# A Gram matrix of split halves from one doubled cross product in place of two

## What is computed

```python
h = relu(einsum('btd,edh->ebth', x, Wd1) + bd1[:, None, None, :])
recon = einsum('ebth,ehd->ebtd', h, Wd2) + bd2[:, None, None, :]
losses = mean((recon - x[None]) ** 2, axis=(2, 3))
idx = argmin(losses, axis=0)       # one expert of 8 for each batch
```

## Time and profile before

| | before |
| --- | --- |
| median of 3 runs | 2398.17 us (2398.06 to 2401.6) |
| the profiled execution's own time | 2398.65 us |
| its span, first to last instruction | 2396.9 us |
| mean granted TensorE clock | 0.972 |
| PE busy | 2142.2 us, 89% |
| DVE busy | 1480.8 us, 62% |
| ACT busy | 995.4 us, 42% |
| POOL busy | 661.0 us, 28% |

### The profile page before, as it was taken

One profiled execution on the slowest core, in us unless ns is written; L12 is line 12 of the kernel. 1 busy time (PEld: TensorE's weight loads), 2 busy tenths in 40 slices (PEclk: granted clock), 3 DMA queues, 4 the chain that ended last, 5 costly groups with the idle time before them and its releaser, 6 DMA issues.

```text
span 2396.9 us, 62050 instructions
## 1 busy us (share of the span) xinstructions
PE 2142.2 (89%) x26607; PEld 1403.2 (59%) x26607; DVE 1480.8 (62%) x3341; ACT 995.4 (42%) x1746; POOL 661.0 (28%) x902
## 2 busy tenths in 40 slices
PE   1589999999999999999999999999999999999955
PEld 1354756657475665747566574756657475565724
DVE  4466666575666667566666756666675666666531
ACT  1335344453534445354444535444453544445220
POOL 2112142231414223141322314132231413222041
PEclk9889999999999999999999999999999999999978
DMA  3312021120302103030210303021030302102010
GB/s 75 77 29 72 11 80 37 33 76 11 107 11 79 38 29 80 11 107 11 79 39 26 83 11 107 11 78 40 27 82 11 107 11 77 41 24 68 11 36 18
DMA packets 99866, 117.35 MB, mean 49 GB/s; under 512 B 19916, under 2 KB 70613, under 8 KB 99575
## 3 DMA queue, kind: packets, MB, share of 16 engines
q1 hardware_dynamic: 99592, 113.39, 17.8%
HBM read 36.99 MB, written 16.78 MB: 22 GB/s over the span
## 4 chain that ended last, share of the span: by engine, by line
PE 67%; DVE 13%; SPq 6%; ACT 6%; issue 3%; POOL 2%; DMA 1%; DVEq 1%; POOLq 0%; ACTq 0%
PE NS L865 10%; PE ringF L1081 10%; PE ringA L763 8%; PE ringF L1066 7%; SPq L373 6%; PE KV L946 5%; PE ringA L1032 5%; PE ringF L1114 3%; PE ringA L908 2%; DVE stage L1505 2%; PE ringA L932 2%; PE ringF L763 2%; PE ringF L1116 2%; ACT E L620 2%; PE ringF L1062 2%
## 5 line engine op out<-in xcount | busy, mean ns | idle before, releaser
L1081 PE MATMUL ringF<-x,H 128*128 128x257 f16 x1536 | 261.0, 273 | 0.0
L1429 DVE TENSOR_REDUCE mx<-ringA 128x8 f32<-128x512 f32 x256 | 175.6, 686 | 114.4 <-PE ringA L908 114.1
L1081 PE MATMUL ringF<-H 128*128 128x128 f16 x1536 | 233.7, 220 | 1.4 <-DVE H L1516 1.4
L612 ACT ACTIVATE E<-ringA,score_scale 128x512 f32<-128x512 f32 x256 | 175.3, 685 | 117.9 <-PE ringA L932 117.9
L763 PE MATMUL ringA<-xT,wqkv 128*128 128x512 f16 x768 | 177.9, 382 | 18.2 <-DMA KS<-KS 11.8
L620 ACT ACTIVATE E<-ringA,score_scale 128x512 f32<-128x512 f32 x256 | 158.6, 684 | 76.0 <-PE ringA L963 76.0
L1066 PE MATMUL ringF<-wd,x2T 128*128 128x512 f16 x768 | 190.0, 384 | 0.0
L1482 DVE SCALAR_TENSOR_TENSOR X<-X,NS 128x320 f32<-128x320 f32 x160 | 78.1, 488 | 180.7 <-PE NS L865 175.5
L1415 DVE TENSOR_REDUCE mx<-ringA 128x1 f32<-128x512 f32 x256 | 162.7, 684 | 31.3 <-PE ringA L899 31.0
L427 POOL TENSOR_SCALAR vtmp<-mv,eps_ffn 128x8 f32<-128x8 f32 x16 | 5.1, 316 | 628.1 <-DVE mv L1261 628.1
L427 POOL TENSOR_SCALAR vtmp<-mv,eps_ln 128x8 f32<-128x8 f32 x32 | 9.9, 310 | 608.6 <-DVE mv L1261 594.6
(11 more groups left out here) (251 smaller groups left out, 4634.2 us busy)
## 6 DMA issues: line engine op xcount, KB each, us to landing
KS<-stage SPq DMA_DIRECT2D x384, 64.0 KB, 2.0
QS<-stage SPq DMA_DIRECT2D x384, 64.0 KB, 2.0
xin<-in_L_attn_x_dram SPq DMA_DIRECT2D x16, 1024.0 KB, 6.8
xres<-in_L_attn_x_dram SPq DMA_DIRECT2D x16, 1024.0 KB, 7.9
out_dram<-yout SPq DMA_DIRECT2D x16, 1024.0 KB, 5.4
QS<-LB SPq DMA_DIRECT2D x16, 512.0 KB, 4.4
E<-in_L_attn_w_qkv_dram SPq DMA_DIRECT2D x1, 768.0 KB
E<-in_L_ffn_Wd_dram SPq DMA_DIRECT2D x2, 256.0 KB
```

Source lines behind the costliest of these rows:

```text
L612: A(E[:, k % ESLOTS, :], ps[:, :], ACT.Exp, scale=score_scale[:, 0:1]).then_inc(freed["s3"].sem, 1)
L1081: ins = MM(dst, H[:, a, t, own], src, start=first and i == 0, stop=last and i >= 4, skip_group_check=True)
L1429: V_.reduce_max(mx1[:, t, 8 * h:8 * h + 8], take(b, "m1", k)[:, :].rearrange("p (a m) -> p a m", a=8), AX.X)\
```

## The change

`H` gets a third plane. DVE's `hidden` gets a second instruction, which writes twice the high half there, and signals a new semaphore. PE's `gram` drops the matmul high by low, and in the matmul low by high the right operand is the doubled plane. PE waits once for the new semaphore, at the first tile of q = 0. As the sum against a symmetric matrix is the same for a matrix and its transpose, twice one cross product gives what the two gave.

```diff
-        H = sb("H", [P, 2, T, EH], F16)
+        H = sb("H", [P, 3, T, EH], F16)
...
+        h2 = sig("h2", T)
...
             def gram(b, q, tiles):
                 if q == 0 and 0 in tiles:
                     pe.wait_ge(freed["h"].sem, freed["h"].at(b, T))
+                    pe.wait_ge(h2.sem, h2.at(b, T))
...
-                            (0, ps[:, 0:P], H[:, 0, t, own]), (0, ps[:, 0:P], H[:, 1, t, own]),
+                            (0, ps[:, 0:P], H[:, 0, t, own]),
                             (0, ps[:, P:GR], x16[:, 0, t, 0:C + 1]), (0, ps[:, P:GR], x16[:, 1, t, 0:C + 1]),
-                            (1, ps[:, 0:P], H[:, 0, t, own]), (1, ps[:, P:GR], x16[:, 0, t, 0:C + 1]))):
-                        ins = MM(dst, H[:, a, t, own], src, start=first and i == 0, stop=last and i >= 4, skip_group_check=True)
+                            (1, ps[:, 0:P], H[:, 2, t, own]), (1, ps[:, P:GR], x16[:, 0, t, 0:C + 1]))):
+                        ins = MM(dst, H[:, a, t, own], src, start=first and i == 0, stop=last and i >= 3, skip_group_check=True)
...
                 V_.scalar_tensor_tensor(out=H[:, 1, t, :], in0=bank("h", t)[:, :], scalar=0.0, in1=H[:, 0, t, :],
                                         op0=ALU.max, op1=ALU.subtract).then_inc(freed["h"].sem, 1)
+                V_.tensor_scalar(H[:, 2, t, :], H[:, 0, t, :], 2.0, None, ALU.mult).then_inc(h2.sem, 1)
```

## The result

The changed kernel takes 2374.92 us (median of 4 runs, 2372.74 to 2376.48) against 2398.11 us before: a ratio of 0.9904, 95% interval 0.9891 to 0.9916, that is 20 to 26 us less. The forecast was 2378.4 us, 19.7 us less.

What follows compares the result with a forecast made beforehand. PE, busy 89%, was taken as the likely limit, but not in every stage. A gain of 25.1 us less a cost of 5.3 us gave 19.8 us, so 2378.4 us against the runs' median; range 2369 to 2386 us.

Steps and rivals of the forecast that it cites:

- Price of the removed matmul: PE's gram: each removed short matmul saves 0.0555 us by the spacing of starts, a half of four tiles 0.222 us.
- 81 ns for each removed pair: Rival in PE's gram: weight loads set the pace, so 36.6 us gained and 2366.9 us in all; chance 0.03.
- Seven halves of eight: Gram halves in 15 batches: all but the first half of gram(0) shorten the path, 23.3 us.
- covered half: First half of gram(0), ahead of the values' transposes: PE only waits longer for DVE, 0.46 not 0.24 us; no gain.
- Slack under the other halves: Iteration stage: the chains over DVE and ACT have 1.09 and 1.49 us spare against 0.22 us removed.
- Price of the added instruction: DVE's doubling of 128x512 f16: 285 ns long, by the slope of the f16 copy.
- step d: Time one doubling adds to DVE's stream: 0.20 us, with bounds 0.09 and 0.40.
- f32 rate: Rival on DVE's doubling: d is 0.40 us, cost 11.5 us, 2384.6 us in all; chance 0.09.
- Where it meets the path: Maxima stage: only hidden(4) with 0.14 us and hidden(7) with 0.20 us delay PE, 0.34 us a batch, 5.1 us.
- small waits at k = 4 and 5: Sign in the maxima stage: new small PE waits for DVE's reduction (L1429) appear there.
- The tail: After the last batch: 32 removed matmuls save 1.8 us, the last doubling ahead of the gram costs 0.2 us.
- The clock: Drops between 2.4 and 1.2 GHz in 13 of 15 batches may shift: -8.5 to +1.3 us, in the range only.

Runs made afterwards that it cites:

- doubled variant: The changed kernel with a second doubling of tiles 4 and 7 alone, into spare memory; 2382.8 us, ratio 0.9934 to the kernel before.
- kernel before with 5 and 3 tiles: The kernel before with the first pair's gram cut 5 and 3 tiles around the values' transposes, not 4 and 4; 2391.6 us, ratio 0.9971.
- DVE part alone: The kernel before with the doubled plane written and waited for, but all six matmuls a tile kept; 2401.3 us, ratio 1.001.
- two doublings moved: The changed kernel with the doublings of tiles 4 and 7 moved to places where DVE waits for PE; 2371.7 us, ratio 0.9886.
- the one with POOL: The changed kernel with all eight doublings given to POOL behind norm2, none on DVE; 2375.2 us, ratio 0.9906.

## Why the prediction was right

- **Price of the removed matmul.** 0.0555 us each and 0.222 us a half were predicted, so 1.55 us for seven halves; the iteration is 1.56 us shorter. After the change a tile's five matmuls start within 0.445 us. The order of time on PE shows one tile, from 1104.04 to the start of the next at 1104.49:

```profile
1104.04 0.23 PE L1083 MATMUL ringF<-H 128*128 128x128 f16 x1
1104.11 0.38 PE L1083 MATMUL ringF<-x,H 128*128 128x257 f16 x2
1104.33 0.22 PE L1083 MATMUL ringF<-H 128*128 128x128 f16 x1
1104.38 0.27 PE L1083 MATMUL ringF<-x,H 128*128 128x257 f16 x1
1104.49 0.22 PE L1083 MATMUL ringF<-H 128*128 128x128 f16 x1
```

  At 81 ns for each removed pair the seven halves would have given 28 x 0.081 = 2.27 us. That rival, taken from the Trainium skill (TensorE: Matmul & The Clock Gate, Back-to-back issue gap), is refuted for this stream, and its lone gap of 56 ns is what the stream shows.
- **Seven halves of eight.** Right: the wait at the values' transposes went from 0.24 to 0.46 us in 15 batches, and giving the covered half its matmuls back cost nothing.
- **Slack under the other halves.** Right: no wait for ACT or DVE appears inside the iteration. PE waits for ACT at L866 three times in all, at L865 before four times, and all of these lie in the first body, which has no gram.
- **Price of the added instruction.** 285 ns from the slope of the f16 copy, 282 measured; the step d of 0.20 us held in the doubled variant. The f32 rate, the rival with d = 0.40, is out. The estimate of 290 ns from the Trainium skill (VectorE: DVE Perf Modes, The perf-mode tier table, with the fixed term from Side-by-side: where the cycles go for N=2048 bf16) is 3% over the measured duration.
- **Where it meets the path.** 0.34 us a batch predicted, 0.36 measured; two of eight instructions count, as the moved and the doubled variants show. One sign was announced wrongly: the small waits at k = 4 and 5 don't appear among PE's waits. The starts show the push all the same: L932 from k = 4 to k = 5 before takes 1.14 us (1084.43 to 1085.57), L933 after takes 1215.71 - 1214.46 = 1.25 us. An idle time shorter than a matmul's modelled tail isn't listed.
- **The tail.** Right in its two terms. The gram takes 14.29 us after and 16.10 before, 1.81 less for 1.8 predicted, and the wait ahead of it 1.66 against 1.41 us, 0.25 more for 0.2. A third part was not in the sum: the twelve adapter matmuls behind the choice of the expert, which the prediction let move along unchanged. They run in part at the lower clock, and take 5.28 us before, 4.46 after and 2.78 in the kernel before with 5 and 3 tiles. The stretches that hold them, in this order (us, busy and count of PE, PEld, DVE, ACT, POOL, then the clock):

```profile
2362.30:2367.70 5.40, 5.28 (x12) 1.91 (x12) 0.03 (x1) 0.78 (x2) 0.00 (x0) 0.52 0.00 0
```

```profile
2340.90:2345.50 4.60, 4.46 (x12) 1.77 (x12) 0.07 (x2) 0.77 (x1) 0.00 (x0) 0.63 0.00 0
```

```profile
2357.40:2360.20 2.80, 2.78 (x12) 1.24 (x12) 0.00 (x0) 0.77 (x1) 0.00 (x0) 1.00 0.00 0
```

  The second profiles of the two kernels have 5.24 and 4.37 us, so 0.8 to 0.9 us of the gain come from here.
- **The clock.** The premise that failed. I gave a range of -8.5 to +1.3 us on the ground that 13 of 15 batches had a drop and that a changed period would shift them. A second profile of the same kernel had 8 with the same span. The drops are scatter between executions of one program and no property of the kernel before. Nor is 0.65 us a fixed price: the two rows give 140.02 - 139.32 = 0.70 us, and the batches with a drop in all profiles are between 0.4 us and, where other waits come in, over 2 us longer than the shortest ones. That the result lies inside the range does not bear this term out.
- **The sum.** 25.1 - 5.3 = 19.8 us. The second profiles of the two kernels are 2396.9 - 2376.6 = 20.3 us apart, the first ones 22.2. The runs say 23 us with an interval of 20 to 26, so the forecast lies just beyond its edge, some 3 us short. Eight of the eleven kernels lie 2 to 4 us below the sum of their stages, the DVE part alone too (2.7 us slower and not 5.6). The one with two doublings moved is within 1 us of it, the kernel before with 5 and 3 tiles too, and the one with POOL is about 2 us above. The runs of one kernel taken together scatter by 1.4 to 7.1 us. Of the 3 us, 0.8 to 0.9 stand in the tail's adapter, as shown above; what the rest is stayed open.

## What to carry to other kernels

Price a removed matmul by the distance of starts in the stream, and an added one-input DVE instruction by the slope of its own type and memories. Then ask for each instruction separately what waits behind it: here 28 of 32 removed ones counted in a batch and 2 of 8 added ones did, and moving these two took the whole cost away. When a removal only lengthens a wait, that wait is a place for work: two more tiles moved into it gained another 15 us, the second of them although it pushed what waited there, because a second wait behind it still set the pace.

## What the runs showed of the hardware

- Idle time ahead of a matmul in the profile counts from the modelled end of the one before, which lies 0.16 us after the point at which PE could go on (0.27 us long, 0.11 us spacing). A listed wait of 0.24 us was room for 0.40 us, and a place with no listed wait had 0.19 us.
- A f16 tensor_scalar of 128x512 in SBUF takes 282 ns on DVE and 1.49 us on POOL; eight of them on POOL didn't lengthen the DVE instructions that ran beside them (reductions, statistics and those that read PSUM). The 2.40 us of the earlier trace rows were of another kind, a scalar_tensor_tensor with its tensors in SBUF beside a tensor_tensor of POOL; no instruction of that kind ran beside a doubling.
- The granted clock fell to its lower level after the same stretch of the batch in 6 to 13 of 15 batches, in different numbers for the same program (13 and 8); where nothing else comes in, a batch with a drop is 0.4 to 0.7 us longer than the shortest.
- Twelve matmuls of 512 columns in the tail took 5.28 us at a mean granted clock of 0.52, 4.46 at 0.63 and 2.78 at 1.00.
